# Three orders of work in a four-layer kernel: an output product behind the next scores, a one-column GELU ahead of a wait, and GpSimd's sums ahead of its scales

## What is computed

```python
x = x + _layernorm(_L0_attn_ref(_layernorm(x), ...))   # windowed sigmoid attention, 16 heads of 8
x = x + _layernorm(_L0_ffn_ref(_layernorm(x), ...))    # softmax attention over 8 batches, then 8 experts, each token takes one
x = x + _layernorm(_L1_attn_ref(_layernorm(x), ...))   # convolution, selective scan, gate, projection
x = x + _layernorm(_L1_ffn_ref(_layernorm(x), ...))    # silu gate, two gelu layers 512x512, projection

# _L0_attn_ref
tau = jax.nn.sigmoid(jnp.einsum('bthd,bthwd->bthw', q, nb_k) / SCALE)
msg = jnp.einsum('bthw,bthwd->bthd', tau, nb_v)
y = x + msg.reshape(B, T, D) @ wo.T
return layernorm(y) * gamma + beta

# _L0_ffn_ref, the experts
he = jax.nn.gelu(flat @ w1[e].T + b1[e], approximate=False)
oe = he @ w2[e].T + b2[e]
out = jnp.where((assign == e)[:, None], oe, out)
```

## Time and profile before

| | |
|---|---|
| runs | 908.96 us median of 3 (899.03 to 910.29) |
| profiled execution | 912.69 us, of which the span from first to last instruction is 910.9 us |
| PE busy | 782.0 us (86%) |
| PEld busy | 661.9 us (73%) |
| DVE busy | 655.5 us (72%) |
| ACT busy | 586.7 us (64%) |
| POOL busy | 441.0 us (48%) |
| granted TensorE clock, mean | 0.917 |

### The profile page before, as it was taken

How to read it: one execution, slowest core, us unless ns; L and a number is a source line. 1 busy time by engine, 2 the same in 40 slices (tenths; PEclk the granted TensorE clock), 3 DMA queues, 4 the chain that set the end, 5 groups by cost and what they waited for, 6 DMA issues and landing times.

```text
span 910.9 us, 21586 instructions
## 1 busy us (share of the span) xinstructions
PE 782.0 (86%) x8256; PEld 661.9 (73%) x8256; DVE 655.5 (72%) x1974; ACT 586.7 (64%) x1118; POOL 441.0 (48%) x776
## 2 busy tenths in 40 slices
PE   4978863899999999878768679999999999989996
PEld 4877752789989898867546457777778777767885
DVE  3587763777999999763699958686776867775532
ACT  4586861356767676746787569595867949555641
POOL 2477664233656565455588735436353533434101
PEclk9997985559999999999786889999999999999998
DMA  8400001200000000000000000000000000000000
GB/s 271 146 26 20 21 19 51 56 1 2 3 2 3 2 3 2 2 2 1 1 1 0 1 1 1 1 1 13 1 13 1 2 11 1 13 0 12 13 1 24
DMA packets 22406, 16.95 MB, mean 19 GB/s; under 512 B 2848, under 2 KB 20640, under 8 KB 22048
## 3 DMA queue, kind: packets, MB, share of 16 engines
q1 hardware_dynamic: 21296, 14.95, 5.4%
q10 hardware_dynamic: 1008, 0.63, 0.3%
HBM read 11.38 MB, written 4.19 MB: 17 GB/s over the span
## 4 chain that ended last, share of the span: by engine, by line
PE 56%; DVE 20%; ACT 9%; POOL 8%; issue 6%; DMA 1%; ACTq 0%; POOLq 0%; SPq 0%; DVEq 0%
PE ps L1716 9%; PE ps L1718 8%; PE ps L1717 8%; PE ps L1729 7%; PE ps L1796 6%; PE ps L2161 3%; DVE wall L1375 3%; PE ps L1735 2%; PE ps L1711 2%; PE ps L2020 2%; ACT tau L706 1%; ACT hbd L688 1%; PE ps L1789 1%; PE ps L2074 1%; PE ps L1820 1%
## 5 line engine op out<-in xcount | busy, mean ns | idle before, releaser
L1716 PE MATMUL ps<-h_h,wh_h 128*128 128x512 f32 x256 | 106.2, 415 | 1.4 <-DVE raw L1514 1.2
L1718 PE MATMUL ps<-h_l,wh_h 128*128 128x512 f32 x256 | 101.0, 395 | 0.0
L1717 PE MATMUL ps<-h_h,wh_l 128*128 128x512 f32 x256 | 100.8, 394 | 0.0
L1796 PE MATMUL ps<-w_e,he 128*128 128x128 f32 x512 | 78.2, 286 | 12.7 <-ACT he L738 12.3
L1796 PEld LDWEIGHTS ps<-w_e,he 128*128 128x128 f32 x512 | 67.0, 196 | 17.4 <-ACT he L738 16.9
L1729 PEld LDWEIGHTS ps<-mov,hbd 32*128 32x128 f32 x2048 | 77.7, 230 | 1.3 <-issue 1.3
L1729 PE MATMUL ps<-mov,hbd 32*128 32x32 f32 (+1 forms) x2048 | 76.8, 306 | 1.0 <-issue 1.0
L584 POOL TENSOR_TENSOR term<-term 128x224 f32<-128x224 f32 (+2 forms) x48 | 37.9, 790 | 79.0 <-DVE term L1406 76.5
L738 ACT ACTIVATE he<-ps,pp 128x256 f32<-128x256 f32 x128 | 58.6, 472 | 21.2 <-PE ps L1718 19.7
L1514 DVE SCALAR_TENSOR_TENSOR raw<-ps,pp,gate 128x512 f32<-128x512 f32 x32 | 23.8, 749 | 49.5 <-ACT gate L921 49.3
L1375 DVE TENSOR_TENSOR wall<-dec,wall 128x224 f32<-128x224 f32 (+6 forms) x112 | 48.7, 435 | 14.6 <-ACT dec L876 11.3
(11 more groups left out here) (299 smaller groups left out, 2522.8 us busy)
## 6 DMA issues: line engine op xcount, KB each, us to landing
x<-in_x SPq DMA_DIRECT2D x16, 128.0 KB
w_h<-in_w_h SPq DMA_DIRECT2D x2, 1024.0 KB, 8.0
x<-x SPq DMA_DIRECT2D x16, 128.0 KB, 1.8
xB<-x SPq DMA_DIRECT2D x32, 64.0 KB
out_x<-xB SPq DMA_DIRECT2D x32, 64.0 KB
w_m<-in_w_m SPq DMA_DIRECT2D x3, 256.0 KB, 3.5
stage_negsel<-in_c_negsel SPq DMA_DIRECT2D x1, 512.0 KB, 4.9
xB<-in_w_e SPq DMA_DIRECT2D x1, 512.0 KB, 6.0
```

The costliest lines, as they stand in the source:

```text
L1716: pe.matmul(dst, a_h, b_h, start=start, stop=True, skip_group_check=True)
L1717: pe.matmul(dst, a_l, b_h, start=False, stop=True, skip_group_check=True)
L1718: return pe.matmul(dst, a_h, b_l, start=False, stop=True, skip_group_check=True)
L1796: last = pe.matmul(ps[:, ACC, P * c:P * c + P], he[e % 2][:, P * c:P * c + P], w_e2[:, e, :], start=False, stop=True, skip_group_check=True)
```

## The change

```diff
+        gelu_one = sb("gelu_one", [P, 1])
...
     gpsimd step_c(n, have):
+                if entering is not None and n < NB:
+                    input_scale(entering)
                 if have(-2):
                     c_ln2.rstd_and_shift(pool, chain, eps, half, minus, (n - 2) % 4, n - 1)
                 if n == NB:
-                    input_scale(block_of(n, 4))
+                    input_scale(entering)
                     c_ln2.rstd_and_shift(pool, chain, eps, half, minus, (NB - 1) % 4, NB)
-                elif entering is not None:
-                    input_scale(entering)
                 if leaving is not None:
                     output_scale(leaving)
                 if have(0):
                     sums(n)
-                if have(4):
+                odd = n >= 5 and n % 2 == 1
+                if have(4) and not odd:
                     scales(n + 4)
                 if have(0):
                     skips(n)
                 if have(-2):
                     stored(n - 2)
+                if have(4) and odd:
+                    scales(n + 4)
...
     scalar step_b(n, q, have):
                 if have(0):
+                    act.activation(gelu_one[:, :], half[:, 0:1], ACT.Gelu)
                     gelu(n, l, 2)
                     gelu(n, l, 3)
...
     tensor step_a(n, l, have):
                             if j == NBLK - 1 and g % 2 == 1:
                                 last.then_inc(S["a_s_ps"], 1)
+                if have(-1):
+                    pe.wait_ge(S["a_msgT"], n)
+                    out_tokens(4 * o + 3, msgT[o], wa[:, 3, :], S["a_y_ps"])
                 if have(1):
                     pe.wait_ge(S["a_xl"], n + 2)
                     project(o, 4 * o, wa_h, wa_l, S["a_qk_ps"], S["a_v_ps"])
...
                     last.then_inc(S["a_m_ps"], 1)
-                    pe.wait_ge(S["a_msgT"], n + 1)
-                    out_tokens(4 * l + 3, msgT[l], wa[:, 3, :], S["a_y_ps"])
```

## The result

The changed kernel takes 954.2 us (median of 4 runs, 948.0 to 958.3) against 906.0 us of the kernel before (899.0 to 910.3): the ratio is 1.054, interval 1.050 to 1.058. It is slower by about 48 us. The forecast was 946 us with a range of 924 to 962.

A forecast was written before the change was run, and what follows sets the result against it. Bounds: two equal loops in stage one, VectorE's order in stage two, a nearly gapless TensorE in stage three. 912.7 (profiled) + 41 + 2 - 1.7 - 4.5 = 949.5, less 3.7 to the median: 946 us, range 924 to 962.

The forecast's parts named there:

- The loop: Stage one: two side-by-side loops become one; a step takes 8.98 us at full clock, 11.20 at the lower, against 6.34.
- The clock: Stage one: the granted clock falls in most steps and is low for most of the scores; about 10.5 us a step, +41 us.
- two thirds: Stage one: chosen share of the 2.22 us between full-clock and lower-clock step, added to 8.98 us.
- 2 us for the casts: Stage one: chosen addition for casts of weights in steps 6 to 8 and a late t_y of sequence 15.
- 0.20 for each of ten such steps: Stage two: VectorE's only gap, 0.20 us ahead of xl, is given back in each of ten steps, -2.0 us.
- -1.7: Stage two, the GELU: whole term in us, from -2.0, perhaps -0.5 and up to +0.8; bounds +3.2 and -7.6.
- The price of the load: Stage two, ScalarE: a table load takes 1.28 us with no drain ahead of it, starting when the Exp ends.
- GpSimd's order: Stage three: c_ya comes some 2.4 us earlier, ending TensorE's waits for it in three steps; -4.5 us, between 0 and 7 gained.
- Clock low throughout: Rival, stage one: the clock stays low through the whole stage, +50.4 us there, 955 us in all; chance 0.16.
- The later stages giving all that TensorE waited: Rival, stages two and three: they gain 7.6 and 7 us, stage one as forecast, 937 us; chance 0.12.
- Clock up: Rival, stage one: the clock stays up, +21.6 us there, +17.4 in all, 926 us; chance 0.12.
- The faster case: Rival, stage one: scores start where the output product stood, xl does not hold them; gains 9 us, 894 us; chance 0.04.

The follow-up runs named there:

- filled kernel: Changed kernel with 32 small matmuls of no use added on TensorE behind each sequence's messages in stage one, where TensorE otherwise waits for xl: 936.1 us, ratio 1.024 to 1.038.

## Why the prediction was right, and where its sizes were off

**The loop: right, and shown.** The step that carried the forecast was that the two loops of stage one become one. The filled kernel has it at full clock with 8.97 us for a predicted 8.98. At the lower clock 11.20 were predicted, and six steps of the changed kernel took 11.1 to 11.2 us (23.99 to 34.78 was 10.79, then 45.97 and 57.16, 11.19 each). Shortening the VectorE part shortened the step as much: 8.97 to 6.92 for vT and xl moved.

**The clock: right in sign, too small.** I took two thirds of the way from 8.98 to 11.20, with 2 us for the casts: 138.5 us for the stretch. It was 143.6, 11.04 us a step. The steps with casts, 12.93 and 12.13 us, were 2.7 us above 11.2 together; of the remaining steps most were at the lower level, 9.8 us at the least. The mis-sized term is "two thirds": without these 2.7 us the share was (10.84 - 8.98) / 2.22 = 0.84. It is not known more closely than that: the kernel with the TensorE edit alone took 139.8 us for the same stretch, which gives 0.72. The reason given for the fall, some 3 us idle in one piece in each step (2.33 and 3.17 in the rows above), was there. A share of two thirds was right for the time: a granted clock of 0.67 in the mean is the lower level for two thirds of the stretch. But the steps of 11.19 us, which pay the full price, had 0.58 to 0.66 in the mean. It was enough that the scores and the output product, the part of the loop on TensorE, fell into the low part. The idle time did not grow with a fall: it was 2.33 us ahead of the scores at 57.16, behind a step of 11.19 us, and 3.17 behind the one of 9.80.

**The GELU: the step that failed is "0.20 for each of ten such steps".** I had seen that VectorE's row had no gap but the one ahead of xl, and concluded that filling it shortens the row. The row contained an instruction whose length was itself a wait, the copy, and it grew by the 0.29 us. The interval of the edit alone (-4.4 to +0.4 us) holds the -1.7, but the mechanism gave 0.0 a step. The price of the load was right: 1.28 us, starting 0.02 us behind the Exp (301.54 to 301.56). The Trainium skill, ScalarE: Activation LUTs, section "What ACT_TABLE_LOAD costs", has about 1380 ns of drain on top of the load. This trace does not agree: the load begins 0.02 us behind the Exp, and the next ACTIVATE 0.02 us behind the load.

**GpSimd's order: right by its chain, too small by 3 us.** The same two steps in the timeline of the changed kernel, to be laid beside the earlier trace rows:

```profile
657.23 0.84 POOL L599 TENSOR_TENSOR xB<-xB,c_r 128x256 f32<-128x256 f32 x1 [0.53 <-ACT c_r L132]
661.57 0.55 POOL L570 TENSOR_TENSOR c_ve<-c_ln_mv,eps 128x2 f32<-128x2 f32 x1 [3.50 <-DVE c_ln_mv L111]
...
664.19 0.86 DVE L108 BATCH_NORM_STATS2 d_ln_st<-xB 128x6 f32<-128x128 f32 x4
...
668.47 1.25 DVE L140 TENSOR_SCALAR d_xn<-xB,d_ln_mv,d_ln_rs 128x128 f32<-128x128 f32 x4 [1.27 <-POOL d_ln_rs L118]
669.02 0.91 PE L2080 MATMUL ps<-prod,ones 32*128 32x384 f32 x4
```

Against the pair products (620.81 before, 669.02 here, 48.21 apart) the residual sum now ends 7.55 us earlier (658.07 against 617.41 + 48.21; the prediction had 7.7), the statistics of the block begin 1.46 us earlier and without a wait (predicted 1.32), and d_xn 2.50 us earlier (predicted 3.0). The wait of 5.64 us for the scales is 3.50, and the residual sum is no longer queued behind it. All three waits for c_ya went. But I took 4.5 where these waits alone were 5.0, for fear of another wait that did not come; the three blocks in which they stood became shorter by 1.6, 2.2 and 1.8 us, 5.6 in all, and 1.6 more came from the clock.

**The sum.** Against the forecast of 36.8 us (43 - 1.7 - 4.5) the two profiled executions differ by 41.0: 5.4 us more in stage one's stretch, 2.4 more between it and stage two, 0.5 and 3.0 less in the stages behind. The errors partly cancel, and the stretches of single executions carry a spread of their own: the old order of stage one took 89.8 to 98.5 us in seven kernels. That the median came within 8 us of 946 is in part luck. Of the 4 us that are left of these 8, 3.7 are my step from the profiled execution to the median: the changed kernel's profiled execution, with 1.9 us around its span 953.8, lay at its median.

**The rivals.** Clock low throughout, 955 us, is nearest to the median of 954.2; it had 0.16. In mechanism the run lies between it and the forecast, with a share of 0.72 to 0.84 between 0.67 and 1. The later stages giving all that TensorE waited, 14.6 us: they gave 9.7 us in the profiled pair, none of it in the steady step of stage two. Clock up, 926 us: the filled kernel (936) shows that even with work in the wait it falls in some steps. The faster case, scores not held by xl, needed t_y to xl in 3.5 us; with 4.06 us in the kernel with vT and xl moved the result was still no faster than before.

## What to carry to other kernels

Before a product is moved behind work of the next item, look at who reads it first and what that engine has to do before the moved work's successor can start: a wait of 0.8 us a step was free here because two loops of equal length ran side by side, and joining them cost 2.6 us a step at full clock and 3.7 with the clock. When a loop must cross an engine, put the instruction that closes it (here xl, with vT in front of it) ahead of the statistics that nobody waits for yet; that gave back 43 of the 54 us. And before a gap is counted as a gain, see whether an instruction behind it changes its length with what another engine does.

## What the runs showed of the hardware

- A VectorE copy of 128x16 that takes 0.13 to 0.17 us elsewhere took 0.61 when it began 0.15 us after a GpSimd instruction of 0.72 us, and ended 0.03 us behind it, in each of ten steps and in each kernel with the hoisted load and the copy.
- 32 bf16 matmuls of 128 columns a step, with no use, made its stretch in stage one 15.8 us shorter; the granted clock over it rose from 0.67 to 0.87.
- One row group's share of the scores takes as long alone (1.96 us) as four interleaved (1.98 us).
- Stretches that no edit touched differ by several us from one kernel's execution to the next: stage one from 1 to 14 took 89.8 to 98.5 us in kernels with the old order, and the fifth step of stage two 14.9 to 18.3 us in three kernels that leave that stage as it was, with the clock low in the longest and up in the shortest. An edit worth 2 us is read from its steady step, not from the total.
- The granted clock of the views reads 1.00 for the first 34 us of both kernels, yet the output product took 1.22 us at 27.68 in the changed kernel and 1.23 at 33.90 in the kernel before, against 0.71 at full clock. There the rows tell the pace, and the means of 0.67 and 0.93 are a little too high.
